# Node rows stored in the order of the edges, in a graph network of four layers

## The chip, the cores and the metric

The kernel runs on one core of a Trainium2 chip. The metric is the device time of one execution in microseconds (us). The engines are PE (matrix products), DVE (vector), ACT (activations), POOL (here above all the issuer of indirect DMAs) and SP, which issues plain DMAs. Data lies in HBM, and passes through SBUF (128 partitions) and PSUM.

## The reference

50,000 nodes with 256 numbers each, and 50,000 edges (src, dst), sorted by dst. Four layers follow each other, each with a residual and a layer norm.

```python
edge_index = jnp.stack([src, dst])
x = _layernorm(x + _L0(x, edge_index, edge_weight, W, b))        # 2 hops: msg = segment_sum(norm * h[src], dst); relu(h) @ W.T + b
x = _layernorm(x + _L1(x, ..., edge_attr_3, edge_index))         # attention over 8 heads, edge encoder dotted with h[dst]
x = _layernorm(x + _L2(x, edge_attr_64, src, dst, ...))          # attention, score = eh[src] + ee + et[dst]
x = _layernorm(x + _L3(x, edge_attr_20, ..., edge_index))        # filter, below
# L3: row, col = ei (so row = src and col = dst)
filt = silu(rbf @ Wf1 + bf1) @ Wf2 + bf2
agg = segment_sum(x[col] * filt, row)                            # x[dst], summed by src
h = silu(agg @ Wu1 + bu1) @ Wu2 + bu2
return x + (gamma * (h - mean) * rsqrt(var + 1e-5) + beta)       # mean and var over all nodes
```

## The kernel before

Nodes and edges are padded to NP = 128 x 392 and laid out as [P, C]: partition p holds C = 392 neighbouring rows. Every stage walks over the columns, G = 2 columns a slot (196 slots) or, in the attention, G = 4 columns a unit (98 units), through 4 or 7 buffers. Since edges are sorted by dst, the sum over the edges of one node is a running sum along a partition, and a small fix-up joins runs that cross partitions.

The stages are separate blocks with a barrier between them:

- `setup` (L153): loads, index vectors, degrees. Its last block (L360) works out `last_i`, the row of each node's last edge, and writes a small table beside x (`XT`, L436).
- `hop_edges(0)`, `hop_edges(1)` (L440): POOL gathers a row per edge (L480), DVE adds along the column (L541), SP stores the running sums.
- `layer_nodes(0..2)` (L622): for each node POOL gathers the finished sum by `last_i` (L673), SP loads x (L663), DVE adds bias, mixes and measures, ACT applies the norm (L616), PE turns and multiplies for the next table (L833). In layers 1 and 2 DVE first inverts the 16 denominators of a slot (L701, L705).
- `attention_edges(1)`, `(2)` (L844): for each of 4 columns POOL gathers the row of dst (L901) and that of src (L903). SP at step t issues the attributes of t (L877), the store of unit t-2 (L883), and a write of zeroes to one of the two tables that the filter adds into (L887); all are on one queue. DVE at step t scores t (L971 to L989; in layer 2 from L977) and sums t-1 (L1000 to L1007). PE encodes the attributes (L916), ACT rectifies and takes exponentials (L933).
- `filter_edges` (L1081): POOL gathers x[dst] (L1116) and, three slots later, adds messages into A[0] and A[1] by src (L1123); each pair of adds waits until that of the slot before has landed. Edges of one column with equal src are first joined by a product with an equality matrix (`eq`, L1195, and L1160 on PE); all but the first go to a trash row. PE computes the filter (L1137, L1151) and turns the src column (L1143), DVE compares and multiplies (L1195 to L1215).
- `update_nodes` (L1220): SP loads both tables, DVE adds them (L1300), PE turns and multiplies twice.
- `finish_nodes` (L1322): batch norm on ACT (L1368), x loaded by SP (L1343), sum, layer norm, store.

An engine executes its instructions in the order in which `unrolled` writes them: at step t each stage function in the list runs for slot t - lag. `hold(e, *done(stage, i, s, back))` waits until `stage` has finished the slot `back` before this one.

## Time and profile before

| what | value |
|---|---|
| median of 3 runs | 8170.37 us (8163.16 to 8176.74) |
| profiled execution | 8169.49 us |
| its span | 8167.8 us |
| busy share: PE, DVE, ACT, POOL | 52%, 65%, 40%, 58% |
| mean granted TensorE clock | 0.713 |
| HBM read, written | 968.89 MB, 840.95 MB |

The span runs from the first to the last instruction. A busy share is a mean over the stages, which have different limits, so a table by stage says more; its rows stand below. "DMA share" is the mean busy share of the 16 DMA engines, and PEld is PE's loading of weights. The first group shows eight stages, one a line: setup, attention 1, node stage 1, attention 2, node stage 2, filter, update, finish; in brackets stands how many instructions ran.

### The profile page before, as it was taken

To read this page: it belongs to the slowest core of one execution; us is meant where nothing else is said; L and a number is where in the kernel's file an instruction comes from. 1 tells how busy PE (TensorE), PEld (TensorE's weight loads), DVE (VectorE), ACT (ScalarE), POOL (GpSimd) and SP (SyncE) were. 2 spreads that over 40 slices of the span, in tenths; PEclk is the share of its full clock that TensorE was granted. 3 is DMA by queue.
4 is the path that set the end of the run, shared out by engine and by line. 5 is a ranking of instruction groups with operands and counts; after the bars stand their busy time and mean duration, and the time that the engine had idled before them with its cause. 6 is when DMAs were issued, how large, how long until landed. Compare 5 with 4: busy or idle time off the path is not lost. (4 is left out here: it accounts for less than half of the span.)

```text
span 8167.8 us, 82421 instructions
## 1 busy us (share of the span) xinstructions
PE 4280.0 (52%) x18128; PEld 3266.2 (40%) x18128; DVE 5331.3 (65%) x16616; ACT 3287.2 (40%) x8834; POOL 4767.5 (58%) x4730
## 2 busy tenths in 40 slices
PE   7800000799963333488511111003877877999854
PEld 4400000688852222366411111002555554888733
DVE  7856677677767777799744446997444444455577
ACT  4567300688851111388500001443222222444499
POOL 7777677544447777566577776666777777000000
PEclk9955555899975555699855555556888887999955
DMA  9299899777767677799755556886555554666699
GB/s 273 7 279 311 291 301 299 234 243 243 243 194 222 221 222 224 231 357 357 258 179 179 177 178 187 270 270 182 83 83 84 84 84 77 197 203 203 203 361 348
DMA packets 1128113, 1764.26 MB, mean 216 GB/s; under 512 B 247612, under 2 KB 606500, under 8 KB 1127626
## 3 DMA queue, kind: packets, MB, share of 16 engines
q1 hardware_dynamic: 641162, 903.37, 33.4%
q0 software_dynamic: 238720, 537.64, 26.8%
q10 hardware_dynamic: 247744, 318.00, 11.2%
q8 instruction: 154, 2.52, 0.1%
q14 instruction: 333, 2.73, 0.1%
HBM read 968.89 MB, written 840.95 MB: 222 GB/s over the span
## 5 line engine op out<-in xcount | busy, mean ns | idle before, releaser
L673 POOL DMA_INDIRECT st<-S,last_i x1176 | 1152.3, 980 | 872.8 <-DVE yt L714 364.7
L903 POOL DMA_INDIRECT rows<-T,src_i x784 | 749.4, 956 | 238.9 <-issue 238.9
L616 ACT ACTIVATE xo<-z,shift,rsd 128x256 f32<-128x256 f32 x1568 | 849.9, 593 | 0.5 <-issue 0.2
L1123 POOL DMA_INDIRECT A<-comb,ai x392 | 628.8, 1604 | 161.7 <-issue 135.7
L916 PE MATMUL psE<-encs,attr 4*128 4x256 f32 x784 | 369.7, 648 | 620.0 <-DMA attr<-in_attr3T 617.8
L933 ACT ACTIVATE psX<-diff 128x40 f32<-128x40 f32 x196 | 40.7, 208 | 1592.4 <-DVE diff L989 1592.4
L916 PE MATMUL psE<-fes,attr 64*128 64x8 f32 x784 | 183.3, 360 | 804.4 <-DMA attr<-in_attr64T 802.1
L1137 PE MATMUL psH<-rbf,wf1s 20*128 20x256 f32 x784 | 264.7, 464 | 603.3 <-DMA rbf<-in_rbfT 603.3
L1195 DVE TENSOR_SCALAR eq<-psI,src_f 128x128 f32<-128x128 f32 x392 | 136.8, 349 | 668.9 <-DMA A<-comb,ai 597.5
L565 PE MATMUL psC<-sums,chain 128*128 128x256 f32 x4 | 2.4, 700 | 1082.6 <-PEq L454 1082.6
L588 DVE BATCH_NORM_STATS2 row_stats<-z 128x6 f32<-128x256 f32 x1568 | 561.3, 400 | 0.1
L916 PEld LDWEIGHTS psE<-encs,attr 4*128 4x128 f32 x784 | 243.7, 325 | 745.7 <-DMA attr<-in_attr3T 686.7
L916 PEld LDWEIGHTS psE<-fes,attr 64*128 64x128 f32 x784 | 174.2, 325 | 813.8 <-DMA attr<-in_attr64T 811.5
L480 POOL DMA_INDIRECT rows<-XT,src_i x392 | 380.6, 971 | 171.1 <-issue 102.1
L1151 PE MATMUL psF<-wf2s,hid 128*128 128x256 f32 x1568 | 477.3, 460 | 0.0
L1116 POOL DMA_INDIRECT rows<-X,dst_i x392 | 391.0, 997 | 136.5 <-issue 118.8
L901 POOL DMA_INDIRECT rowsd<-T,dst_i x392 | 371.4, 947 | 168.2 <-issue 107.6
L480 POOL DMA_INDIRECT rows<-S,from_i x392 | 396.0, 1010 | 122.9 <-issue 100.3
L833 PE MATMUL psV<-w2s,xT 128*128 128x272 f32 x1568 | 407.7, 403 | 106.8 <-ACT tt L769 106.8
L1182 ACT COPY comb<-psM 128x512 f32<-128x512 f32 x196 | 114.9, 586 | 863.1 <-PE psM L1160 863.1
L901 POOL DMA_INDIRECT rowsd<-ET,dst_i x392 | 373.4, 952 | 149.4 <-issue 118.5
L565 PEld LDWEIGHTS psC<-sums,chain 128*128 128x128 f32 x4 | 1.0, 312 | 1083.3 <-issue 1083.3
(241 smaller groups left out, 14232.2 us busy)
## 6 DMA issues: line engine op xcount, KB each, us to landing
X<-xo ACTq DMA_DIRECT2D x588, 256.0 KB
xt<-X SPq DMA_DIRECT2D x588, 256.0 KB
S<-sums SPq DMA_DIRECT2D x196, 544.0 KB, 3.1
S<-sums SPq DMA_DIRECT2D x392, 256.0 KB, 3.9
A<-zero SPq DMA_DIRECT2D x196, 512.0 KB, 4.6
T<-tt ACTq DMA_DIRECT2D x196, 280.0 KB
T<-tt ACTq DMA_DIRECT2D x196, 272.0 KB
XT<-in_x SPq DMA_DIRECT2D x1, 50176.0 KB, 169.4
```

The costliest lines, as they stand in the source:

```text
L480: e.indirect_dma_start(rows[s][:, k, :], None, table, bass.IndirectOffsetOnAxis(ap=at_i[:, c:c + 1], axis=0))\
L588: ins = e.bn_stats(row_stats[s][:, k, :], z[s][:, k, :])
L616: ins = e.activation(y[s][:, k, :], z[s][:, k, :], ACT.Identity, bias=shift[s][:, k, :], scale=rsd[s][:, k, :])
L673: e.indirect_dma_start(st[s][:, k, :], None, sums_table, bass.IndirectOffsetOnAxis(ap=last_i[:, c:c + 1], axis=0))\
L833: mm = e.matmul(psV[k][:, 0:DW], xT[s][:, k, m * P:(m + 1) * P], weights[:, m, :], start=m == 0, stop=m == K - 1)
L901: e.indirect_dma_start(rowsd[s][:, k, :], None, dtable, bass.IndirectOffsetOnAxis(ap=dst_i[:, c:c + 1], axis=0))\
L903: e.indirect_dma_start(rows[s][:, k, :], None, table, bass.IndirectOffsetOnAxis(ap=src_i[:, c:c + 1], axis=0))\
L916: mm = e.matmul(psE[s % 2][:, k * EW:(k + 1) * EW], attr[s][:, k, :], weights[:], start=True, stop=True)
L1116: e.indirect_dma_start(rows[s][:, k, :], None, X3, bass.IndirectOffsetOnAxis(ap=dst_i[:, c:c + 1], axis=0))\
L1123: e.indirect_dma_start(A[k], bass.IndirectOffsetOnAxis(ap=ai[s][:, k, :], axis=0), comb[s][:, k, :], None, compute_op=ALU.add).then_inc(si ...
L1137: mm = e.matmul(psH[s % 2][:, m * G * P:(m + 1) * G * P], wf1s[:, m * P:(m + 1) * P], rbf[s][:].rearrange("p g q -> p (g q)"), start=True, ...
L1151: mm = e.matmul(psF[s % 2][:, k * D:(k + 1) * D], hid[s][:, m, k * P:(k + 1) * P], wf2s[:, m, :], start=m == 0, stop=m == K - 1)
```

## The change

Node rows are renumbered. Node v, where it has edges, is stored at the row of one of its own edges (the first in the tables between the hops and layer 1, the last from layer 1 on), and nodes without edges fill the rows that are left over. The sums of a node then already lie at the node's row: a stage over the nodes loads them plainly. In exchange x has to be brought into the order: it is gathered in node stage 0 (`input_i`), moved from first to last row in node stage 1 (`turn_i`), and taken back to the nodes' own order in `finish_nodes` (`node_i`). Which empty node takes which free row is worked out by a new block in `setup`, on DVE: for each of the two lists a `compress` (ten binary steps over 392 and ten over 784 numbers) and an `expand` (ten steps over 1568).

```diff
+                        def compress(j, flag, count):
...
+                            for b in reversed(range(BITS)):
+                                link(e.tensor_scalar(bit[:], rem[:], float(2 ** b), None, ALU.is_ge))
+                                e.scalar_tensor_tensor(rev[:], bit[:], float(2 ** (BITS - 1 - b)), rev[:], ALU.mult, ALU.add)
+                                link(e.scalar_tensor_tensor(rem[:], bit[:], -float(2 ** b), rem[:], ALU.mult, ALU.add))
...
+                            for b in range(BITS):
...
+                                e.tensor_scalar(moved[:, 0, :], a, top, 0.0, ALU.subtract, ALU.max)
+                                link(e.scalar_tensor_tensor(z, a, top, a, ALU.is_lt, ALU.mult))
+                                link(e.tensor_tensor(z[:, 0:W - d], z[:, 0:W - d], moved[:, 0, d:W], ALU.add))
+                        def expand(j, turn):
...
+                            for b in reversed(range(BITS)):
...
+                                e.tensor_scalar(moved[:], a[:], top, 0.0, ALU.subtract, ALU.max)
+                                link(e.scalar_tensor_tensor(z[:], a[:], top, a[:], ALU.is_lt, ALU.mult))
+                                if d < W:
+                                    link(e.tensor_tensor(z[:, :, d:W], z[:, :, d:W], moved[:, :, 0:W - d], ALU.add))
```

(W = 2 x 392. `link` makes DVE wait for the instruction before the next.) The table beside x gets two more columns, and the hops walk from the last column to the first.

The row of dst is no longer gathered per edge. In attention 1 the stored rows are loaded plainly, ACT sets those that are not at a first edge to zero, and DVE carries the row of the first edge along; the filter does the same from the last edge backwards. In attention 2 the 8 numbers are loaded once for all columns, multiplied, and spread by 8 scans at the start.

```diff
# attention_edges
+                        def take(i, s):
+                            hold(e, *done(spread_, i, s, NS - 1))
+                            e.dma_start(rowsd[s][:], nodes(T1)[:, bass.ds((i * NS + s) * G, G), :]).then_inc(signal(taken, s), 16)
+                        written(N, NS, ([(take, 0)] if layer == 1 else []) + [(stage, 0), (store, 2), (empty, 2)])
...
-                                e.indirect_dma_start(rowsd[s][:, k, :], None, dtable, bass.IndirectOffsetOnAxis(ap=dst_i[:, c:c + 1], axis=0))\
...
+                        def cut_rows(i, s):
+                            hold(e, *done(taken, i, s))
+                            for k in range(G):
+                                ins = e.activation(rowsd[s][:, k, :], rowsd[s][:, k, :], ACT.Copy, scale=isfirst[:, bass.ds((i * NS + s) * G + k, 1)])
...
+                        def spread_rows(i, s):
+                            hold(e, *done(cut, i, s))
+                            for k in range(G):
+                                c = (i * NS + s) * G + k
+                                last = rowsd[s][:, k - 1, :] if k else rowsd[(s - 1) % NS][:, G - 1, :] if i + s else head[:]
+                                ins = e.scalar_tensor_tensor(rowsd[s][:, k, :], last, notfirst[:, c:c + 1], rowsd[s][:, k, :], ALU.mult, ALU.add)
...
-                        written(N, NS, ([(rectify, 0)] if layer == 1 else []) + [(exponentials, 0), (keep_max, 0)])
+                        written(N, NS, ([(cut_rows, 0), (rectify, 0)] if layer == 1 else []) + [(exponentials, 1), (keep_max, 1)])
...
-                        written(N, NS, [(score, 0), (add, 1)])
+                        written(N, NS, ([(spread_rows, 0)] if layer == 1 else []) + [(score, 0), (add, 1)])
```

The filter adds into four tables instead of two: slot s uses A[0], A[1] when it is even and A[2], A[3] when it is odd, and each add waits for the same column two slots back. Each attention stage writes two tables of zeroes where it wrote one. The update loads four tables and adds them in pairs, in three sums a slot for one.

```diff
# filter_edges
-                            hold(e, *done(added, i, s, 1))
                             for k in range(G):
-                                e.indirect_dma_start(A[k], bass.IndirectOffsetOnAxis(ap=ai[s][:, k, :], axis=0), comb[s][:, k, :], None,
-                                                     compute_op=ALU.add).then_inc(signal(added, s), 16)
+                                hold(e, *done(added[k], i, s, 2))
+                                e.indirect_dma_start(A[s % 2 * 2 + k], bass.IndirectOffsetOnAxis(ap=ai[s][:, k, :], axis=0), comb[s][:, k, :], None,
+                                                     compute_op=ALU.add).then_inc(signal(added[k], s), 16)
-                        unrolled(R, NS, [(gather, 0), (add, LAG)])
+                        unrolled(R, NS, [(add, 0)])
...
-                        unrolled(R, NS, [(column, 0), (activate, 0), (copy, 2)])
+                        unrolled(R, NS, [(column, 0), (cut_rows, 0), (activate, 0), (copy, 2)])
-                        unrolled(R, NS, [(compare, 0), (multiply, 1)])
+                        unrolled(R, NS, [(spread_rows, 0), (compare, 0), (multiply, 1)])
# layer_nodes
-                            e.dma_start(xt[s][:], xin[:, c, :]).then_inc(signal(loaded, s), 16)
+                            e.dma_start(st[s][:], nodes(sums_table)[:, c, :]).then_inc(signal(loaded, s), 16)
...
+                        def cut(i, s):
+                            hold(e, *done(st_["weighed"], i, s))
+                            own = islast[:, bass.ds(i * (G * NS) + s * G, G)].rearrange("p (g h) -> p g h", h=1).to_broadcast([P, G, H])
+                            e.tensor_tensor(den[s], den[s], own, ALU.mult).then_inc(signal(st_["cut"], s), 1)
# update_nodes
+                            e.dma_start(third[s][:], nodes(A[2])[:, c, :]).then_inc(signal(loaded, s), 16)
+                            e.dma_start(fourth[s][:], nodes(A[3])[:, c, :]).then_inc(signal(loaded, s), 16)
...
-                        unrolled(R, NS, [(add, 0), (copy, 0), (measure, 3)])
+                        unrolled(R, NS, [(add, 0), (copy, 1), (pair, 0), (measure, 4)])
# finish_nodes
-                            e.dma_start(xt[s][:], nodes(X3)[:, bass.ds(i * (G * NS) + s * G, G), :]).then_inc(signal(loaded, s), 16)
+                                e.indirect_dma_start(xt[s][:, k, :], None, X3, bass.IndirectOffsetOnAxis(ap=node_i[:, c:c + 1], axis=0))\
```

## Rows read from the trace of the kernel before

**Rows 1.** Stages: length; busy PE, PEld, DVE, ACT, POOL; clock; DMA share; GB/s

```profile
0.00:421.00 421.00, 331.18 (x1204) 184.08 (x1204) 321.35 (x862) 206.01 (x395) 316.49 (x410) 0.94 0.59 137
...
2364.00:3394.00 1030.00, 377.19 (x816) 250.29 (x816) 737.29 (x1595) 143.66 (x395) 752.53 (x789) 0.50 0.68 214
3394.00:4015.00 621.00, 495.38 (x2352) 381.36 (x2352) 594.13 (x2156) 500.91 (x1569) 367.41 (x389) 0.98 1.01 344
4015.00:5041.00 1026.00, 190.85 (x816) 180.83 (x816) 494.16 (x1391) 40.18 (x200) 750.85 (x789) 0.50 0.56 172
5041.00:5633.00 592.00, 0.00 (x0) 0.00 (x0) 583.95 (x2156) 250.66 (x588) 368.02 (x390) 0.50 0.85 265
5633.00:6945.00 1312.00, 1025.27 (x3528) 704.89 (x3528) 589.10 (x2156) 298.76 (x785) 1019.80 (x784) 0.83 0.51 82
6945.00:7720.00 775.00, 765.80 (x3920) 673.90 (x3920) 383.82 (x784) 329.57 (x784) 0.00 (x0) 0.99 0.63 200
7720.00:8168.00 448.00, 218.22 (x784) 140.10 (x784) 339.77 (x1378) 426.87 (x982) 0.00 (x0) 0.50 0.98 345
```

**Rows 2.** Groups of instructions: busy, mean ns of one | idle before, releaser

```profile
L903 POOL DMA_INDIRECT rows<-T,src_i x784 | 749.4, 956 | 238.9 <-issue 238.9
L1123 POOL DMA_INDIRECT A<-comb,ai x392 | 628.8, 1604 | 161.7 <-issue 135.7 <-DMA A<-comb,ai 20.4 <-ACT comb L1182 5.7
...
L541 DVE SCALAR_TENSOR_TENSOR sums<-sums,same,rows 128x256 f32<-128x256 f32 x784 | 381.0, 486 | 21.6 <-issue 0.6
...
L496 ACT ACTIVATE xe<-rows,f 128x256 f32<-128x256 f32 x392 | 177.8, 500 | 91.3 <-DVE f L526 89.3
...
L701 DVE TENSOR_SCALAR psDen<-st 128x16 f32<-128x16 f32 x392 | 68.6, 175 | 12.7 <-DMA st<-S,last_i 12.7
```

**Rows 3.** Timeline (start us, length us) of the end of setup

```profile
387.88 0.57 DVE L408 TENSOR_TENSOR ahead<-ahead,w_sb 128x392 f32<-128x392 f32 x1
...
394.25 0.36 DVE L416 TENSOR_SCALAR g_dst<-ahead 128x392 f32<-128x392 f32 x1
...
421.74 1.20 POOL L480 DMA_INDIRECT rows<-XT,src_i  x1 [52.00 <-PEq L454]
```

**Rows 4.** Timeline of a unit of attention 1: score begins, last sums, next attributes usable

```profile
2801.56 1.23 DVE L971 TENSOR_TENSOR enc<-psE,rowsd 128x1024 f32<-128x1024 f32 x1 [3.61 <-DMA rows<-T,src_i]
...
2807.79 1.55 DVE L1007 SCALAR_TENSOR_TENSOR sums<-sums,same,rows 128x264 f32<-128x264 f32 x3
...
2814.49 2.07 PE L916 MATMUL psE<-encs,attr 4*128 4x256 f32 x4 [7.79 <-DMA attr<-in_attr3T]
```

**Rows 5.** DMA issues in attention 1: count, size, median us from issue to landing

```profile
S<-sums SPq DMA_DIRECT2D x74, 544.0 KB, 3.5
A<-zero SPq DMA_DIRECT2D x74, 512.0 KB, 4.7
```

**Rows 6.** Timeline of a unit of attention 2: the same three points

```profile
4501.98 0.19 DVE L977 TENSOR_TENSOR dot<-rows,rowsd 128x32 f32<-128x32 f32 x1 [5.66 <-DMA rows<-T,src_i]
...
4505.67 1.55 DVE L1007 SCALAR_TENSOR_TENSOR sums<-sums,same,rows 128x264 f32<-128x264 f32 x3
...
4513.17 1.02 PE L916 MATMUL psE<-fes,attr 64*128 64x8 f32 x4 [9.04 <-DMA attr<-in_attr64T]
```

**Rows 7.** Timeline of a slot of the filter, DVE and PE

```profile
6202.31 0.35 DVE L1195 TENSOR_SCALAR eq<-psI,src_f 128x128 f32<-128x128 f32 x1 [3.90 <-DMA A<-comb,ai]
...
6204.76 0.69 DVE L1215 TENSOR_TENSOR fl<-psF,rows 128x512 f32<-128x512 f32 x1
...
6205.50 1.13 PE L1160 MATMUL psM<-fl,eq 128*128 128x256 f32 x4 [2.76 <-DVE fl L1215]
...
6206.56 1.13 PE L1137 MATMUL psH<-rbf,wf1s 20*128 20x256 f32 x4
...
6207.62 0.43 PE L1143 MATMUL psI<-ident,sc 128*128 128x128 f32 x2
...
6207.89 1.89 PE L1151 MATMUL psF<-wf2s,hid 128*128 128x256 f32 x8
```

More of the change, by code:

```diff
@@ new lines, in setup @@
+                assert W <= 1024 and C < 512
+                rowid, free, empty, frees, empties = [tmp(n, [P, C]) for n in ("rowid", "free", "empty", "frees", "empties")]
+                firsts, lasts = tmp("firsts", [P, C]), tmp("lasts", [P, C])
+                below = tmp("below", [P, 2])
+                deg, ok, dinv, sq = tmp("deg", [P, C]), tmp("ok", [P, C]), tmp("dinv", [P, C]), tmp("sq", [P, C])
+                degr, okr, root = tmp("degr", [P, C]), tmp("okr", [P, C]), tmp("root", [P, C])
@@ L381, in _ @@
                         link(e.tensor_tensor_scan(number[:], unit[:], psNum[:, 0:C], 0.0, ALU.mult, ALU.add))
+                        link(e.tensor_tensor(firsts[:], number[:], psNum[:, 0:C], ALU.subtract))
+                        link(e.tensor_scalar(empty[:], has[:], -1.0, 1.0, ALU.mult, ALU.add))
+                        link(e.tensor_tensor_scan(empties[:], unit[:], empty[:], 0.0, ALU.mult, ALU.add))
+                        link(e.tensor_tensor_scan(frees[:], unit[:], notfirst[:], 0.0, ALU.mult, ALU.add))
                         assert n[0] == NUMBER
@@ L564, in _ @@
                     def _(e):
-                        e.matmul(ps[:], chain[:], sums[NS - 1][:, G - 1, :], start=True, stop=True).then_inc(carried, 1)
+                        e.matmul(ps[:], chainT[:], sums[NS - 1][:, 0, :], start=True, stop=True).then_inc(carried, 1)
                     @block.gpsimd
                     def _(e):
-                        at = bass.IndirectOffsetOnAxis(ap=first_e[:], axis=0)
+                        at = bass.IndirectOffsetOnAxis(ap=start_e[:], axis=0)
                         e.wait_ge(cleared, 1)
@@ L1093, in filter_edges @@
                 psH, psI, psF, psM = [[bank(f"{n}{j}") for j in range(2)] for n in ("psH", "psI", "psF", "psM")]
-                gathered, added, attred = stage_of("gathered", NS, G), stage_of("added", NS, G), stage_of("attred", NS, 1)
+                tail = ctx.enter_context(sbuf("tail", [P, D], F32))
+                taken, attred = stage_of("taken", NS, 1), stage_of("attred", NS, 1)
+                added = [stage_of(f"added{k}", NS, 1) for k in range(G)]
+                cut, spread_ = stage_of("cut", NS), stage_of("spread", NS)
+                csteps, ends = semaphore("csteps"), semaphore("ends")
                 stages = [stage_of(n, NS) for n in (
@@ L1110, in _ @@
+                        unrolled(R, NS, [(take, 0), (stage, 0)])
                     @block.gpsimd
                     def _(e):
-                        def gather(i, s):
-                            hold(e, *done(message, i, s, NS))
-                            for k in range(G):
-                                c = i * (G * NS) + s * G + k
-                                e.indirect_dma_start(rows[s][:, k, :], None, X3, bass.IndirectOffsetOnAxis(ap=dst_i[:, c:c + 1], axis=0))\
-                                    .then_inc(signal(gathered, s), 16)
@@ L1128, in _ @@
+                        unrolled(R, NS, [(add, 0)])
+                        for sem, value in total(added[0], R) + total(added[1], R):
                             e.wait_ge(sem, value)
@@ L1180, in copy, with cut_rows @@
                             hold(e, *done(joined, i, s))
-                            hold(e, *done(added, i, s, NS))
+                            hold(e, *done(added[0], i, s, NS))
+                            hold(e, *done(added[1], i, s, NS))
                             e.copy(comb[s][:].rearrange("p g d -> p (g d)"), psM[s % 2][:]).then_inc(signal(copied, s), 1)
-                        unrolled(R, NS, [(column, 0), (activate, 0), (copy, 2)])
+                        def cut_rows(i, s):
+                            hold(e, *done(taken, i, s))
+                            for k in range(G):
+                                ins = e.activation(rows[s][:, k, :], rows[s][:, k, :], ACT.Copy, scale=islast[:, bass.ds(C - (i * NS + s + 1) * G + k, 1)])
+                            ins.then_inc(signal(cut, s), 1)
+                        unrolled(R, NS, [(column, 0), (cut_rows, 0), (activate, 0), (copy, 2)])
                     @block.vector
@@ L1206, in compare, with spread_rows @@
                             e.tensor_scalar(ai[s][:], cnt[s][:], trash[:], None, ALU.add).then_inc(signal(compared, s), 1)
+                        def spread_rows(i, s):
+                            hold(e, *done(cut, i, s))
+                            for k in reversed(range(G)):
+                                c = C - (i * NS + s + 1) * G + k
+                                last = rows[s][:, k + 1, :] if k < G - 1 else rows[(s - 1) % NS][:, 0, :] if i + s else tail[:]
+                                ins = e.scalar_tensor_tensor(rows[s][:, k, :], last, notlast[:, c:c + 1], rows[s][:, k, :], ALU.mult, ALU.add)
+                                if k:
+                                    ins.then_inc(csteps, 1)
+                                    e.wait_ge(csteps, (i * NS + s) * (G - 1) + G - k)
+                            ins.then_inc(signal(spread_, s), 1)
                         def multiply(i, s):
```

426 lines of the change are left out of this document (322 added, 104 removed).

## The prediction, made before the changed kernel ran

> **What bounds the kernel now.** I read first the table of stages [rows 1], because the stages are separate blocks and each has its own limit. Setup (421 us) is vector work and PE counting. The hops and the first node stage (421 to 2364 us, left out of the rows) are paced by row gathers and by PE; nothing in them is removed. The two attention stages take 1030 and 1026 us, and POOL is busy for 750 us in each although DVE differs by 240 us: POOL sets both. The two later node stages (621 and 592 us) have DVE busy for 594 and 584 us: DVE sets them. The filter stage (1312 us) has POOL busy for 1020 us. The update has PE busy for 766 of 775 us. In finish ACT is busy for 427 of 448 us and the DMA engines move 345 GB/s.
>
> Then I read what one POOL operation costs with its issue gap [rows 2]: a gather is 0.96 us plus 0.30 us of issue, so 1.26 us each; an accumulating scatter is 1.60 plus 0.3 us. An attention unit has 8 gathers: 8 x 1.26 = 10.05 us, and 98 units are 985 us of the 1030. A filter slot has 2 gathers and 2 scatters: 2.5 + 3.9 = 6.4 us, against 1312/196 = 6.7. So the change attacks what really binds there. By the code POOL's indirect DMAs fall from 11 x 392 to 8 x 392, but 392 of those left are new in a stage that had none.
>
> The sum is made against the profiled execution (8169.5 us, 1.7 us of it outside the span); the median shown is 8170.4 us, so no correction is needed. This kernel's timing tells a change from none at about 0.2%, 16 us.
>
> **Setup, +207 us.** A new block works out the free rows, on DVE alone, one instruction waiting for the last. [rows 3] gives the prices: 0.57 us for a two-operand instruction over 392 elements (spaced 0.60), 0.36 us for a one-operand one (0.40). The larger part is loops that compress or spread a list in ten binary steps. I scale with length at about 1.04 ns an element for two operands and half that for one: an estimate from those rows. One compress: 30 instructions over 392 (15 us), 30 over 784 or less (24 us), 8 more (4 us) = 43 us, twice: 86. One expand: 10 steps over 1568 elements (0.9 + 1.8 + 1.6 us) = 43 us and 12 shorter ones (9 us) = 52, twice: 105. The rest, some 45 instructions and the PE round trips, 29 us. That is 220. Added in the older blocks: 20 more instructions, 13 us. Against that, the hop started 27 us after DVE's last instruction, because the small table was still being written [rows 3]; now it is written during the second expand, and those 26 us go. 220 + 13 - 26 = 207. Bounds 185 and 235.
>
> **Hops and node stage 0, 0.** The order of columns is turned round and index copies are three columns wide, with the same gathers of the same bytes. In node stage 0 the gather moves from the sums to x; PE stays full. Bounds -5 and +10.
>
> **Attention 1, +14 us.** Half of the gathers go: POOL needs 5.0 us per unit. What is late next? DVE: from enc to the last sum it takes 2809.34 - 2801.56 = 7.78 us [rows 4], and it gets four carried multiply-adds over 280 elements; three over 264 take 1.55 us, so four take 2.1: 9.95 us per unit. So the relief is nearly nothing here. Beside it, there is a loop through SP's queue. At the end of unit t-2's sum, SP issues the store, then two zero writes (one before), then the load of the rows for t+1. A tiny load behind one store and one zero write was usable at 2814.49, 5.15 us after DVE's end [rows 4]; a store lands 3.5 us after its issue and a zero write, issued some 0.4 us behind it, 4.7 us [rows 5], so each further half megabyte costs 1.6 us. The new load is usable at 5.15 + 1.6 + 1.6 = 8.4 us; ACT then scales four rows, 0.50 us each with some overlap [rows 2]: 10.3 us. DVE's step is 9.95, and the loop spans two steps: (9.95 + 10.3)/2 = 10.1, I take 10.2. 97 x 10.2 + 55 (what the stage has outside its units now) = 1044. Bounds -10 (9.95) and +125.
>
> The Trainium skill (DMA: Bandwidth & Descriptors, Queues, rings and completion order) says that descriptors of one queue are consumed in ring order on each engine; the late tiny load agrees. Were the load free to pass the writes, the unit would be DVE's 9.95 us and the stage 1020.
>
> **Attention 2, -249 us.** No carried rows here: the destination's 8 numbers are spread once for all. DVE's chain is 4501.98 to 4507.22, 5.24 us [rows 6]; POOL 5.0. But bytes per unit are 0.56 MB gathered, 0.56 stored, 1.05 zeroes, 0.13 attributes, 2.29 MB. Now the stage moves 172 GB/s at a DMA share of 0.56 [rows 1], 307 GB/s at a full share; node stage 1 shows 344 at 1.01. So 2.29 MB take 6.7 to 7.5 us: the engines bind before DVE. The loop: attributes were usable 5.95 us after DVE's end (4513.17) [rows 6], plus 1.75 for the second zero write, plus 1.9 us of PE = 9.6; (5.24 + 9.6)/2 = 7.4 us. 97 x 7.4 + 51 + 8 (the spreading at the start: a multiply and eight scans, partly behind the first gathers) = 777. Bounds 738 (7.0 us) and 870.
>
> **Node stages 1 and 2, +43 us each.** The gathers that go were not binding. DVE gets one small multiply on 16 numbers in PSUM with a wait behind it: the neighbouring 16-number operation takes 0.175 us [rows 2], and wait and drain add 0.04: 0.22 x 196 = 43. Nothing hides it, since DVE is busy for 96 to 99% of both. Bounds 25 and 60 each.
>
> **Filter, -404 us.** POOL keeps two scatters, 3.9 us a slot, and with four tables a scatter waits for the same column two slots back rather than one. Next are PE and DVE. PE's starts in a slot [rows 7]: from join to hide 1.06, hide to transpose 1.06, transpose to filter 0.27, the filter 1.89: 4.28 us. DVE: 6202.31 to 6205.45 = 3.14 us [rows 7], plus two carried adds of 0.485 each [rows 2] = 4.15. The ring of four buffers (compare, the next step's multiply, join, copy, two scatters and a landing) I estimate at 15 us over 4 slots, 3.75 a slot. With three engines within 0.4 us of each other I take 4.5, not 4.3. 196 x 4.5 + 26 = 908. Bounds: 869 (4.3) and 1053 (5.24).
>
> The carried adds have two SBUF inputs, and POOL reads indices from SBUF. The Trainium skill (SBUF — State Buffer, on the port pair shared by DVE and GpSimd) says that such a DVE operation and a GpSimd operation that reads SBUF exclude each other for a whole instruction. In attention 1 now, with such sums on DVE, gathers keep to a mean of 0.96 us [rows 2]. By the rule each scatter could wait 0.5 us, 4.9 us a slot and 986 for the stage; I go by the row.
>
> **Update, +36 us.** Loads double: 1.31 MB per slot with the store, and PE's slot is 3.9 us. By the stage's own rate (200 GB/s at 0.63, 317 at a full share [rows 1]) they take 4.1 us; by node stage 1's 344 GB/s they take 3.8. I take 4.08: 800 + 11 = 811. DVE gets two more sums of 0.68 us (scaled as in setup), 384/196 + 1.4 = 3.4 of 3.9 us in all, and stays below. Bounds 0 and +95.
>
> **Finish, +61 us.** x now comes by 392 gathers at 1.26 us = 494 us; they start with the block, and from the last to the stored row I estimate 14 us: 509 instead of 448. POOL takes ACT's place as the bound. Bounds 50 and 85.
>
> **Sum.** 207 + 14 - 249 + 43 + 43 - 404 + 36 + 61 = -249: 8169.5 - 249 = 7920 us.
>
> **Rivals.** A: the filter doesn't get to 4.5. PE's granted clock is 0.83 there [rows 1], below full speed; if it stays so, 4.28/0.83 = 5.16 us a slot, 1037 for the stage, 8050 in all. For: 0.83 with PE busy 78%. Against: node stage 1 has 0.98 at 80%, and PE would be nearly full.
>
> B, slower than before: the added bytes cost more than the gathers saved. The attention stages get 103 MB more of zeroes, the update 103 MB more of loads. If mixed reading and writing stays at 270 GB/s, attention 1 takes 11.3 us a unit (+107 on my sum), attention 2 8.5 (+107), the update 4.85 (+151), finish 2.9 (+77): 8362. It decides below about 288 GB/s. For: attention 2 manages 307 per full share. Against: node stage 1 and finish show 344 and 345 GB/s in fact.
>
> C: everything sits on its engine's floor, 4.3, 7.0, 9.95 and 3.9 us: 138 us less, 7782.
>
> D: the gathers that go weren't what bound attention 2 and the filter, and the stages keep their length: 8169.5 + 404 = 8573. The 0.30 us gaps between POOL's operations speak against it; I give it 0.02.
>
> **How the numbers follow.** Forecast 0.57, A 0.19, C 0.12, B 0.10, D 0.02. The forecast's own range is 7850 to 8000. The range reaches to C and past A, and into the way to B: 7790 to 8130. Slower: B and D, 0.12. Same: 0.03, the point where B just eats the gain. Faster: 0.85.
>
> **What would show it.** Setup ends near 628 us; enc starts follow each other by 10.2 us in attention 1 and the first dot by 7.4 in attention 2, with DVE waiting for attributes; mix starts 3.25 us apart in node stages 1 and 2; filter slots are 4.5 us with a granted clock near 1 and POOL waiting for comb; POOL is the engine without idle time in finish. I am wrong if setup's chain is spaced otherwise, if the filter waits for its scatters' landing, or if attention 2 stays above 8 us a unit.

## The result, and the profile after

The changed kernel takes 8085.51 us (median of 4 runs, 8070.34 to 8096.18) against 8166.76 us for the kernel before, run beside it (4 runs, 8162.18 to 8176.74): ratio 0.9897, 95% interval 0.9878 to 0.9917. It is faster by 81 us or 1.0%, a third of the 249 us that were forecast, and inside the range. The profiled execution took 8096.18 us, its span 8094.3 us, so its stages add up to 73 us less than before.

The first view is the table of stages of the changed kernel, with the columns of [rows 1] and its order of stages: setup, attention 1, node stage 1, attention 2, node stage 2, filter, update, finish.

```profile
0.00:629.00 629.00, 351.17 (x1244) 194.63 (x1244) 536.97 (x1154) 206.56 (x396) 321.53 (x412) 0.82 0.40 93
...
2579.00:3729.00 1150.00, 377.20 (x816) 250.22 (x816) 934.00 (x1982) 309.13 (x787) 387.70 (x395) 0.50 0.69 236
3729.00:4377.00 648.00, 512.42 (x2352) 367.44 (x2352) 621.64 (x2357) 481.34 (x1569) 370.80 (x392) 0.98 1.00 330
4377.00:5178.00 801.00, 190.80 (x816) 180.78 (x816) 503.74 (x1400) 39.10 (x199) 377.60 (x395) 0.50 0.87 284
5178.00:5817.00 639.00, 0.00 (x0) 0.00 (x0) 621.31 (x2353) 252.22 (x590) 0.97 (x1) 0.50 0.77 247
5817.00:6625.00 808.00, 792.03 (x3528) 592.44 (x3528) 752.76 (x2548) 434.80 (x1176) 613.30 (x392) 0.99 0.80 133
6625.00:7589.00 964.00, 815.04 (x3920) 672.33 (x3920) 619.11 (x1177) 329.41 (x785) 0.00 (x0) 0.97 0.82 267
7589.00:8094.00 505.00, 218.35 (x784) 140.25 (x784) 354.52 (x1378) 437.82 (x982) 371.11 (x392) 0.50 0.94 306
```

Length against [rows 1], in us:

| stage | before | forecast | after | moved by |
|---|---|---|---|---|
| setup | 421 | +207 | 629 | +208 |
| hops and node stage 0 | 1943 | 0 | 1950 | +7 |
| attention 1 | 1030 | +14 | 1150 | +120 |
| node stages 1, 2 | 621, 592 | +43, +43 | 648, 639 | +27, +47 |
| attention 2 | 1026 | -249 | 801 | -225 |
| filter | 1312 | -404 | 808 | -504 |
| update | 775 | +36 | 964 | +189 |
| finish | 448 | +61 | 505 | +57 |

Two stages miss badly, attention 1 by 106 us and the update by 153. The filter gives 100 us of it back: without that luck the kernel would take some 8185 us, outside the range and slower than before. In the two stages that miss no engine is full: DVE is busy for 934 of 1150 us, PE for 815 of 964, and the DMA engines for 0.69 and 0.82. So a wait sets them. The timelines show which. First a unit of attention 1 after (start, length, idle before it and its releaser):

```profile
3002.82 1.55 DVE L1268 SCALAR_TENSOR_TENSOR sums<-sums,same,rows 128x264 f32<-128x264 f32 x3
3003.54 1.78 ACT L1160 ACTIVATE rowsd<-rowsd,isfirst 128x280 f32<-128x280 f32 x4 [6.76 <-DMA rowsd<-T]
...
3003.79 3.78 PE L1143 MATMUL psE<-encs,attr 4*128 4x256 f32 x8 [8.39 <-DMA attr<-in_attr3T]
3004.40 0.33 SPq L1101 DMA_DIRECT2D S<-sums  x1
3004.64 0.94 POOL L1126 DMA_INDIRECT rows<-T,index_i  x1 [5.43 <-DVE sums L1268]
3004.77 1.46 SPq L1106 DMA_DIRECT2D A<-zero  x2
...
3006.27 1.41 SPq L1111 DMA_DIRECT2D rowsd<-T  x1
...
3007.60 1.07 ACT L1154 ACTIVATE psE<-psE 128x512 f32<-128x512 f32 x2 [2.28 <-PE psE L1143]
...
3008.80 1.22 DVE L1232 TENSOR_TENSOR enc<-psE,rowsd 128x1024 f32<-128x1024 f32 x1 [1.18 <-ACT psX L1166]
...
3014.14 1.78 ACT L1160 ACTIVATE rowsd<-rowsd,isfirst 128x280 f32<-128x280 f32 x4 [5.20 <-DMA rowsd<-T]
...
3014.60 3.77 PE L1143 MATMUL psE<-encs,attr 4*128 4x256 f32 x8 [7.04 <-DMA attr<-in_attr3T]
```

POOL idles for 5.43 us, as it should with half of the gathers gone. ACT idles for 6.76 us until the rows of dst have landed. Their load waits on SP's queue for DVE's end (3004.37), then follows the store and both zero writes. It has landed at 3014.14, 9.8 us after DVE's end; over 75 units the median is 9.5 us (8.9 to 10.7). The forecast had 8.4. The attributes of the same unit stand behind the rows on the queue: they reach PE a little later (3014.60 here, 9.9 us after DVE's end in the median). PE and ACT then need 4.9 us to encode and rectify them (3003.79 to 3008.67 for the unit shown), and DVE's score (`enc`, L1232) waits for that: it starts 0.13 us after L1154 has ended, and by the code it is `rectified` that it waits for, though the view names the exponentials.

The update, in the same view:

```profile
7003.65 0.84 ACT L1579 ACTIVATE ht<-psO,bu2s 128x256 f32<-128x256 f32 x2 [0.89 <-PE psO L1550]
...
7004.52 0.52 SPq L1531 DMA_DIRECT2D HT<-ht  x1
7005.08 0.61 SPq L1524 DMA_DIRECT2D agg<-A  x1
...
7005.73 0.45 SPq L1525 DMA_DIRECT2D more<-A  x1
...
7005.92 0.69 DVE L1588 TENSOR_TENSOR agg<-agg,more 128x512 f32<-128x512 f32 x1 [1.70 <-DMA fourth<-A]
...
7006.70 0.43 SPq L1527 DMA_DIRECT2D fourth<-A  x1
```

SP issues the store of slot t-4 the moment ACT has written it (7003.65 + 0.84 = 7004.49), and only then the four loads of a later slot. DVE then waits for the last of them. The view of waits sums this over the 800 us from 6700 to 7500 (us in total, times, longest):

```profile
DVE agg L1588 <- DMA fourth<-A: 277.7, 161, 5.6
```

### The profile page after: what moved, and what is told of

Same layout as the page of the kernel before. It is cut to its first block and busy times, and to the rows that moved or that the text cites. A ratio compares the mean times of both kernels' runs of the same rounds, so it can differ in the third digit from the quotient of the medians.

```text
span 8094.3 us, 85002 instructions
## 1 busy us (share of the span) xinstructions
PE 4133.3 (51%) x18168; PEld 3149.1 (39%) x18168; DVE 6231.1 (77%) x18486; ACT 3581.9 (44%) x9619; POOL 3605.0 (45%) x3559
## 3 DMA queue, kind: packets, MB, share of 16 engines
q10 hardware_dynamic: 247744, 318.00, 11.3%
## 5 line engine op out<-in xcount | busy, mean ns | idle before, releaser
L1126 POOL DMA_INDIRECT rows<-T,index_i x784 | 759.3, 969 | 1080.8 <-DVE sums L1268 895.1
L1644 POOL DMA_INDIRECT xt<-X,node_i x392 | 371.1, 947 | 1095.1 <-POOLq L1711 971.5
L879 POOL DMA_INDIRECT xt<-in_x,input_i x392 | 376.6, 961 | 469.5 <-DVE xb L894 393.4
L801 ACT ACTIVATE sd<-mean_var,epsc 128x2 f32<-128x2 f32 x784 | 238.0, 304 | 582.3 <-DVE mean_var L796 578.6
L879 POOL DMA_INDIRECT xt<-X,turn_i x392 | 370.8, 946 | 251.1 <-DVE xb L894 184.1
L681 POOL DMA_INDIRECT rows<-S,index_i x392 | 401.6, 1025 | 122.8 <-issue 101.1
L959 ACT ACTIVATE yt<-yt,m_half 128x256 f32<-128x256 f32 x392 | 183.2, 532 | 565.2 <-DVE yt L925 565.2
L1160 ACT ACTIVATE rowsd<-rowsd,isfirst 128x280 f32<-128x280 f32 x392 | 174.9, 516 | 582.0 <-DMA rowsd<-T 582.0
L1402 PEld LDWEIGHTS psH<-rbf,wf1s 20*128 20x128 f32 x784 | 130.8, 185 | 722.0 <-DMA rbf<-in_rbfT 644.7
L1588 DVE TENSOR_TENSOR agg<-agg,more 128x512 f32<-128x512 f32 x196 | 135.6, 692 | 346.7 <-DMA fourth<-A 346.0
```

Source lines behind the costliest of these rows:

```text
L681: e.indirect_dma_start(rows[s][:, k, :], None, table, bass.IndirectOffsetOnAxis(ap=at_i[:, c:c + 1], axis=0))\
L801: e.activation(sd[s][:, :, 0], mean_var[s][:, :, 1], ACT.Sqrt, bias=epsc[:]).then_inc(signal(rooted, s), 1)
L879: e.indirect_dma_start(xt[s][:, k, :], None, xin, bass.IndirectOffsetOnAxis(ap=at_i[:, c:c + 1], axis=0))\
L959: ins = e.activation(yt[s][:, k, :], yt[s][:, k, :], ACT.Relu, scale=m_half[:, bass.ds(i * (G * NS) + (s * G + k), 1)])
L1126: e.indirect_dma_start(rows[s][:, k, :], None, table, bass.IndirectOffsetOnAxis(ap=at_i[:, c:c + 1], axis=0))\
L1402: mm = e.matmul(psH[s % 2][:, m * G * P:(m + 1) * G * P], wf1s[:, m * P:(m + 1) * P], rbf[s][:].rearrange("p g q -> p (g q)"), start=True, ...
```

## The experiments

All are edits of the changed kernel except the one that edits the kernel before. They fall into two settings, by what the kernel before took beside them: 8165 to 8167 us (the first setting) or 8587 to 8589 us (the second). Whether the chip makes the setting is taken up at the end. A time without a number of runs is that of a single run. I read the length of a unit or slot from first and last start of one DVE instruction (98 units: divided by 97; 196 slots: by 195). For the changed kernel itself that view says, for attention 1, attention 2, filter and update:

```profile
L1232 DVE TENSOR_TENSOR enc<-psE,rowsd x98: 1223/1224/1226, 2595.1 to 3691.7; 128x1024 f32<-128x1024 f32 x98
L1239 DVE TENSOR_TENSOR dot<-dot,psE x98: 186/186/189, 4404.4 to 5143.3; 128x32 f32<-128x32 f32 x98
L1499 DVE TENSOR_TENSOR fl<-psF,rows x196: 690/692/692, 5827.4 to 6609.6; 128x512 f32<-128x512 f32 x196
L1588 DVE TENSOR_TENSOR agg<-agg,more x196: 682/692/694, 6631.5 to 7572.8; 128x512 f32<-128x512 f32 x196
```

That is 11.31, 7.62, 4.01 and 4.83 us.

**The update's store two slots later.**

```diff
-                        unrolled(R, NS, [(load, 0), (store, 4)])
+                        unrolled(R, NS, [(load, 0), (store, 6)])
```

> Update only: the store of slot t-6 instead of t-4 stands behind the load of t in SP's order, so that a load no longer waits until the result of a slot two steps further on is ready. Theory 'order': the update is 4.85 us a slot because SP is held at the store; it falls to 4.1 or less, the stage from 964 to about 810 us and the run by some 150 us. Rival 'rate': five transfers of 256 KB a slot move at 272 GB/s at most in this mix, whoever issues them; the stage stays at 964 within 10 us.

Measured: 7914.57 us (one run, the kernel before 8166.79 beside it). The same starts in the update:

```profile
L1588 DVE TENSOR_TENSOR agg<-agg,more x196: 671/675/693, 6633.4 to 7388.9; 128x512 f32<-128x512 f32 x196
```

3.87 us a slot instead of 4.83, with every byte as before. From 6640 to 7380 us PE has no idle time and the DMA engines move 338 GB/s:

```profile
6640.00:7380.00 740.00, 740.00 (x3797) 653.05 (x3796) 597.67 (x1140) 318.04 (x758) 0.00 (x0) 1.00 0.98 338
```

So the order on the queue cost 0.96 us a slot, 187 us by the slots (171 by the whole time), and the rate nothing.

**The third and fourth table loaded by ACT's queue**, store as in the changed kernel:

```diff
-                            e.dma_start(third[s][:], nodes(A[2])[:, c, :]).then_inc(signal(loaded, s), 16)
-                            e.dma_start(fourth[s][:], nodes(A[3])[:, c, :]).then_inc(signal(loaded, s), 16)
...
-                        unrolled(R, NS, [(activate, 1), (bias, 2)])
+                        unrolled(R, NS, [(load_more, 0), (activate, 5), (bias, 6)])
```

(`load_more` issues the two loads from ACT.)

> Update only: the third and fourth tables are loaded by ACT, through a second queue, with activate and bias at lags 5 and 6 so that the loads are as early as SP's; the store stays at lag 4 on SP. Theory 'order': ACT's two loads come early but SP's two are still held, 4.5 to 4.85 us a slot, 890 to 960 us. Rival 'one queue': a single queue cannot fill the 16 DMA engines (its share is 0.83), two can; 4.1 us, about 810 us. Rival 'rate': 964 us as after the change.

Measured: 8036.39 us, the update 4.53 us a slot. It gains 0.30 us of 0.96: two loads are free of the store, the other two still stand behind it. The store's place counts, more than the number of queues. (ACT's own work had to move to lags 5 and 6 for this, so the queue is not all that differs.)

**Attention's store and zero writes one unit later.**

```diff
-                        written(N, NS, ([(take, 0)] if layer == 1 else []) + [(stage, 0), (store, 2), (empty, 2)])
+                        written(N, NS, ([(take, 0)] if layer == 1 else []) + [(stage, 0), (store, 3), (empty, 3)])
```

> Attention stages only: store and zero writes of unit t-3 instead of t-2 follow the loads of t in SP's order, so that the load of the next unit's rows is issued one step of DVE earlier. Theory 'loop': the stages are set by the loop store, two zero writes, load, and then ACT or PE; with a step more of distance attention 1 falls to DVE's 10.0 us a unit (1150 to about 1030 us) and attention 2 from 7.7 to the DMA engines' 7.0 (801 to about 735). Rival 'rate': the DMA engines cannot move the bytes faster in this mix; both stages stay within 15 us of 1150 and 801.

Measured: 7769.75 us. Starts in attention 1 and 2:

```profile
L1232 DVE TENSOR_TENSOR enc<-psE,rowsd x98: 1223/1224/1225, 2590.7 to 3553.6; 128x1024 f32<-128x1024 f32 x98
L1239 DVE TENSOR_TENSOR dot<-dot,psE x98: 186/186/189, 4266.5 to 4831.4; 128x32 f32<-128x32 f32 x98
```

Attention 1 is 9.93 us a unit, which is DVE's chain of 9.95 in the forecast; the rows still land 9.6 us after the store is issued, but now a unit earlier than they are needed. Attention 2 is 5.82 us, below the 6.7 to 7.5 that the forecast held for the DMA engines' floor. From 4270 to 4830 us they moved

```profile
4270.00:4830.00 560.00, 176.60 (x756) 167.80 (x757) 470.36 (x1334) 35.60 (x190) 356.49 (x376) 0.50 1.05 387
```

387 GB/s. The stage had never been short of rate.

**Zero writes from ACT's queue**, with the old lag of two:

```diff
-                        written(N, NS, ([(take, 0)] if layer == 1 else []) + [(stage, 0), (store, 2), (empty, 2)])
+                        written(N, NS, ([(take, 0)] if layer == 1 else []) + [(stage, 0), (store, 2)])
...
-                        written(N, NS, ([(cut_rows, 0), (rectify, 0)] if layer == 1 else []) + [(exponentials, 1), (keep_max, 1)])
+                        written(N, NS, ([(cut_rows, 0), (rectify, 0)] if layer == 1 else []) + [(exponentials, 1), (keep_max, 1), (empty, 2)])
```

> The changed kernel with attention's zero writes issued from ACT's queue instead of SP's, same lag of two units, same bytes. Theory (the carried-row load waits behind the zero writes because they are on one queue): attention 1 falls from 11.3 to 10.0 to 10.4 us a unit, attention 2 from 7.6 to 6.9 or less, about 8085 - 110 - 70 = 7905. Rival (the DMA engines are short of rate for those bytes wherever they are issued): 11.3 and 7.6 stay, 8085. Should ACT's own work be held up by its issuing, attention 1 would rise above 11.3.

Measured: 8069.28 us, in the second setting, where the kernel before takes 8587. The starts there:

```profile
L1232 DVE TENSOR_TENSOR enc<-psE,rowsd x98: 1223/1224/1225, 2699.0 to 3689.4; 128x1024 f32<-128x1024 f32 x98
L1239 DVE TENSOR_TENSOR dot<-dot,psE x98: 186/186/189, 4401.9 to 5014.6; 128x32 f32<-128x32 f32 x98
```

10.21 and 6.32 us a unit: with the same bytes and the same lag, taking two writes from the queue ahead of the load gives 1.10 us back in attention 1 and 1.30 in attention 2. Rate can't do that. The changed kernel's 11.31 and 7.62 are from the first setting; that can't make the gain, since the one version measured in both (both stores late, below) takes 9.94 and 5.93 us in the second and 9.93 and 5.83 in the first. The expected 7905 was for the first setting.

**Two tables instead of four**: the filter adds as before (each add waits for the same column one slot back), attention writes one table of zeroes per unit, the update loads two.

```diff
-                                hold(e, *done(added[k], i, s, 2))
-                                e.indirect_dma_start(A[s % 2 * 2 + k], bass.IndirectOffsetOnAxis(ap=ai[s][:, k, :], axis=0), comb[s][:, k, :], None,
+                                hold(e, *done(added[k], i, s, 1))
+                                e.indirect_dma_start(A[k], bass.IndirectOffsetOnAxis(ap=ai[s][:, k, :], axis=0), comb[s][:, k, :], None,
```

> Two tables instead of four, the rest of the change kept: each add waits for the same column's add one slot back, the attention stages write one table of zeroes each, the update loads two tables and adds them once. Theory: the four tables were not what freed the filter (the gathers' going was): a landing of 4.0 us and 0.2 of issue allow 4.2 to 4.5 us a slot, the filter takes 840 to 900 us (808 with four), while the update returns to 775 (from 964), attention 1 to 1030 to 1060 and attention 2 to 700 to 740; the run is about 7800 us. Rival: with one pair in flight the adds wait for each other's landing, 5.9 us a slot or more, the filter is back above 1150 us and the run is no faster than 8050.

Measured: 7851.87 us, faster than the change as it was made. Attention 1 is 10.18 us a unit, attention 2 6.66, the filter 4.76 a slot, the update 3.88. In the filter the wait for the landing of the add before comes back; first the waits from 5630 to 6530 us here, then those of the changed kernel from 5830 to 6600:

```profile
POOL A L1387 <- DMA A<-comb,ai: 230.0, 184, 2.1
PEld psM L1425 <- DVE fl L1499: 145.6, 164, 3.6
```

```profile
POOL A L1387 <- DMA A<-comb,ai: 68.3, 118, 0.7
...
PEld psM L1425 <- DVE fl L1499: 3.1, 12, 0.6
```

The filter missed its expected 840 to 900 us: 929 pass between its first and last start alone. Before, a slot was 6.52 us (6915.6 - 5644.8, by 195), so the rest of the change, the gathers' going above all, is worth 1.76 us a slot and the two extra tables 0.75, 147 us. At their first price (110 us in attention 1, 93 in attention 2, 185 in the update) they lost 241 net; the attention part is queueing only.

**Both cures together**, and with two tables:

> The changed kernel with both cures: attention's store and zero writes three units behind instead of two, the update's store six slots behind instead of four. Theory (both stages were held by what stands ahead of the next load on SP's queue, and the two are separate): the gains add up, attention 1 at 9.9 us a unit, attention 2 at 5.8, filter 4.0, update 3.87, so 8085 - 316 - 171 = 7600 us, 7570 to 7630. Rival (the shortened stages take something from each other, or the single looks were lucky): above 7700. Rival from the forecast (the DMA engines' rate sets attention 2 at 6.7 to 7.5 and the update at 4.1 or more): at least 7790.

> As the run before with both stores late, but with the filter adding into two tables as the kernel before does (each add waits for the same column one slot back, one zero write per attention unit, two loads in the update). It prices the four tables once their queueing is cured. Theory: filter 4.76 instead of 4.0 us a slot (+147 us), attention 2 a little below 5.8 (at most 50 us less), attention 1 at DVE's 9.9, update 3.87: 7600 + 147 - 50 = 7700, 7680 to 7760. Rival (the two extra tables cost as much traffic as they save, as without the cure): within 40 us of the run before.

These ran in the second setting: 7820.94 us (5 runs, 7805.67 to 7822.34), ratio 0.9108 (0.9095 to 0.9120), and 7951.76 us (5 runs), ratio 0.9266 (0.9253 to 0.9278); the kernel before 8586.7 (12 runs). The stages named were as expected (9.94, 5.93, 4.02 and 3.87 us; filter 4.75 with two tables). So, once nothing queues, four tables are worth 131 us, and the filter alone differs. The absolute times missed because of the setting. The first again, beside the changed kernel:

> The changed kernel with both stores late, once more, since the last comparison ran where the kernel before took 8587 us instead of 8167 (its row gathers stalled). Theory: where the kernel before takes about 8167 us, this takes 7600 us (7570 to 7630), ratio 0.931; where it takes about 8587, 7820 again, ratio 0.911.

> The changed kernel itself, beside the run before it on one chip, to compare the two directly. Theory: where the kernel before takes 8167 us, 8085, ratio 0.990; where it takes about 8587, about 8300 (7820 plus 316 and 171), ratio 0.967: the gathers that the change removes are those that stall there.

Measured in the first setting, where the kernel before takes 8164.81 us (9 runs): both stores late 7600.91 (5 runs, 7598.3 to 7612.0), ratio 0.9311 (0.9299 to 0.9324); the changed kernel 8081.98 (4 runs), ratio 0.9897 (0.9882 to 0.9912). The cures add up: 481 us.

**The kernel before with the same lags.**

> The kernel before with the same two lags (attention store and zero write 3 units behind, update store 6 slots behind). Theory: nothing, 8167 within 0.3%, since POOL's eight gathers set both attention stages and PE's 3.9 us the update, and the loads were early enough there. Rival (the lags are a gain of their own, and the cured kernel's win is not that of the change): attention or update shorter by over 30 us.

Measured: 8562.57 us (median of 7 runs) against 8586.7, ratio 0.9973 (0.9960 to 0.9986): 24 us, small but clear, against 481 in the changed kernel. So nearly all of the gain needs the shortened stages. The update is 3.88 us a slot, as in the kernel before. For attention it is less certain: this ran in the second setting alone, where the kernel before left no trace, so which stage gave the 24 us isn't shown.

That run also tells what is different in the second setting. POOL's gathers of dst in attention 1, in the view of [rows 2] (mean 955 ns, 947 in the same group of the kernel before in the first setting):

```profile
L901 POOL DMA_INDIRECT rowsd<-T,dst_i x392 | 374.4, 955 | 306.7 <-DVE sums L1007 146.1 <-issue 111.5 <-POOLq L1408 49.0
```

The issue costs the same, but POOL waits 146.1 us for buffers that DVE hasn't freed (11.6 in the first setting). DVE in turn waits for DMAs before its sums (L1003: 145.8 us in 36 gaps), which it hardly does in the first setting: rows land late. In the finish stage of the run with both stores late it is seen singly:

```profile
7496.09 0.69 DVE L1703 SCALAR_TENSOR_TENSOR z<-xt,psN 128x512 f32<-128x512 f32 x1 [1.58 <-issue]
7503.27 0.69 DVE L1703 SCALAR_TENSOR_TENSOR z<-xt,psN 128x512 f32<-128x512 f32 x1 [3.27 <-DMA A<-comb,ai]
7504.94 0.66 DVE L1703 SCALAR_TENSOR_TENSOR z<-xt,psN 128x512 f32<-128x512 f32 x1
```

Between two sums 7.2 us pass instead of 1.6 to 2.5; a gap of over one and a half medians comes 38 times in 195 steps there, 27 of them over 5 us, and 3 times (none over 5 us) in the same kernel's run in the first setting. Hops, attention before and finish after lose by it (attention 1 before: 11.63 us a unit instead of 10.05; finish after: 577 us between first and last sum instead of 483). The filter and the update don't, and the cured attention hardly does (5.93 for 5.83 us in attention 2).

**The cut of the denominators left out** (so nodes without edges get wrong rows), on top of both late stores:

```diff
-                                  + ([(cut, 0), (mix, 0)] if layer else []))
+                                  + ([(mix, 0)] if layer else []))
```

> As the first of these three, but the small multiplication of the 16 inverted denominators by the has-edges flag (node stages 1 and 2) is left out, so nodes without edges get wrong rows. Theory (the forecast's step: one DVE operation of 0.175 us and its wait, on an engine without idle time): node stages 1 and 2 shorter by 43 us each. Rival (the stages' 27 and 47 us more came from something else, the plain loads or x's gathers): shorter by less than 20 us each.

Measured: 7528.05 us. One DVE instruction of attention 2 and one of the filter, with both stores late and then without the cut:

```profile
L1239 DVE TENSOR_TENSOR dot<-dot,psE x98: 186/186/190, 4268.0 to 4833.2; 128x32 f32<-128x32 f32 x98
L1499 DVE TENSOR_TENSOR fl<-psF,rows x196: 690/691/693, 5517.9 to 6298.5; 128x512 f32<-128x512 f32 x196
```

```profile
L1239 DVE TENSOR_TENSOR dot<-dot,psE x98: 186/186/190, 4239.8 to 4802.6; 128x32 f32<-128x32 f32 x98
L1499 DVE TENSOR_TENSOR fl<-psF,rows x196: 690/691/692, 5444.0 to 6224.8; 128x512 f32<-128x512 f32 x196
```

The first start in attention 2 comes 28 us earlier, which is node stage 1. Node stage 2 lies between the last start in attention 2 and the first in the filter: 684.7 us (5517.9 - 4833.2) and 641.4 us (5444.0 - 4802.6), 43 less.

**The cut folded into the bound**, a version that computes everything:

```diff
+                            e.tensor_scalar(least[:], notlast[:], 1e30, 1e-10, ALU.mult, ALU.add)
...
-                            e.tensor_scalar(den[s], v[:, :, :, HD], 1e-10, None, ALU.max).then_inc(signal(st_["combined"], s), 1)
+                            low = least[:, bass.ds(i * (G * NS) + s * G, G)].rearrange("p (g h) -> p g h", h=1).to_broadcast([P, G, H])
+                            e.tensor_tensor(den[s], v[:, :, :, HD], low, ALU.max).then_inc(signal(st_["combined"], s), 1)
```

> The changed kernel with both stores late, and the cut of the denominators folded into the operation before it: the lower bound 1e-10 becomes a column of numbers that is 1e-10 where a node has edges and 1e30 elsewhere, so the inverse is practically zero there and the multiplication goes. Theory (what a look without that multiplication gave, 28 and 45 us, is all regained, the other operation costs the same 0.175 us): where the kernel before takes 8165 us, 7601 - 73 = 7528, 7510 to 7550. Rival (a second operand from SBUF makes the first operation dearer, by up to what the multiplication cost): 7600.

Measured: 7753.11 us (4 runs, 7745.62 to 7756.72) in the second setting, where the kernel before takes 8588.65, ratio 0.9025 (0.9008 to 0.9043). Against both stores late in that setting (7820.94 us, measured another time) that is 68 us less where 73 were expected. It is the fastest version that computes everything; in the first setting it wasn't run. The operation with a second operand costs what the one-operand one did, 0.174 us:

```profile
L910 DVE TENSOR_TENSOR psDen<-st,least 128x16 f32<-128x16 f32 x392 | 68.4, 174 | 4.0 <-DMA st<-S 4.0
```

## Where the forecast was right, and where it failed

The forecast as a whole failed: 81 us came where it had 249. It failed in attention 1 and in the update, and the cause is the same in both: what stands ahead of a load on SP's queue. That the time lies in the range is luck, since the filter's error of 100 us has the other sign.

**Setup, hops, node stage 0, finish: right.** Counting the dependent DVE instructions and scaling [rows 3] with length gave 207 us for setup; it is 208. Finish is POOL's 392 gathers at 1.26 us, +57 for +61.

**Attention 1: two failed steps, and each is about half of the miss.** The loop through SP's queue over two units is right, but a term is too small and the path is not the longest one.

- *"so each further half megabyte costs 1.6 us. The new load is usable at ... 8.4 us".* It is usable 9.5 us after DVE's end. The price was a difference of two landings [rows 5]. With one zero write less (two tables) the rows are usable after 7.5 us, so a half megabyte costs 2.1 us (0.52 MB at 250 GB/s), and two such on 5.15 make 9.3. Why 2.1 and not 1.6 stays open. With 9.5 in place of 8.4 the forecast's equation gives 10.7 us a unit.
- *"ACT then scales four rows ... 10.3 us"*, after which only DVE's 9.95 follow. The loop doesn't close there but through the attributes, which now stand behind the new load: 9.9 us until PE can start, 4.9 for PE and ACT's rectifying, 0.1, and 7.8 from the score to the last sum, 22.7 us for two units, 11.35 a unit; 11.31 is measured. The sum left this path out. With one zero write the same sum is 7.6 + 4.9 + 0.1 + 7.8 = 20.4, 10.2 a unit, for the measured 10.18; by the path through ACT's scaling it would be the 9.95 of DVE.

The fall-back in that paragraph, DVE's 9.95, was right (9.93 with the late store). Its upper bound, +125, held 120. The Trainium skill's rule named there, that descriptors of one queue are taken in ring order (DMA: Bandwidth & Descriptors, Queues, rings and completion order), agrees with the run that issued the zero writes from another queue: 10.21.

**Update: the failed step is "by the stage's own rate they take 4.1 us ... I take 4.08".** I priced only bytes over rate. The rate was even better than I took (338 GB/s, all loads inside PE's 3.87 us). What I left out was the order on SP's queue, for which I had the code: a store that waits for its result stands ahead of the next loads. Before, two loads had time enough behind it, and with two tables and the same lag the slot is 3.88 us again; with four, issued one after another (the fourth starts 1.6 us after the first) and landing behind 0.26 MB of store, they come late. The stage got 189 us longer, twice my upper bound.

**Attention 2: right in its loop, wrong in its floor.** -225 for -249, and 7.62 for 7.4 us a unit. The loop through SP's queue was the right limit and nearly the right size: attributes at PE 8.0 us after the store's issue (7.7 forecast), 2.0 for PE, 5.25 for DVE, half of which is 7.6. The floor beside it, 6.7 to 7.5 us by rate, does not exist: the late store ran at 5.82, close to DVE's 5.24.

**Filter: mechanism right, size off by 100 us.** PE became the bound, at a granted clock of 0.99, so rival A is refuted. The term "PE: 4.28 us" was too large, mostly because its last part took the filter's modelled length (1.89) for the distance to the next start. In the changed kernel:

```profile
6202.63 1.03 PE L1425 MATMUL psM<-fl,eq 128*128 128x256 f32 x4
...
6203.59 1.13 PE L1402 MATMUL psH<-rbf,wf1s 20*128 20x256 f32 x4
...
6204.64 0.43 PE L1408 MATMUL psI<-ident,sc 128*128 128x128 f32 x2
...
6204.91 1.89 PE L1416 MATMUL psF<-wf2s,hid 128*128 128x256 f32 x8
...
6206.64 1.10 PE L1425 MATMUL psM<-fl,eq 128*128 128x256 f32 x4
```

From 6204.91 to 6206.64 are 1.73 us, 0.16 less, and from join to hide (6202.63 to 6203.59) 0.96 instead of 1.06; the whole slot is 4.01. The 0.2 us that I added because three engines were close to each other never came: DVE has 0.49 us of carried adds twice and still keeps up. Its 4.15 us a slot were too many as well; it is busy for 753 us of the stage, 3.8 a slot. The exclusion that the Trainium skill describes (SBUF — State Buffer, SBUF: two separate sides) isn't seen here. 392 scatters took 1.565 us on average beside the carried adds, 1.604 before [rows 2], and single ones overlap them without either getting longer:

```profile
6206.41 1.55 POOL L1387 DMA_INDIRECT A<-comb,ai  x1 [0.30 <-issue]
6206.47 0.47 DVE L1486 SCALAR_TENSOR_TENSOR rows<-rows,notlast,rows 128x256 f32<-128x256 f32 x1
```

```profile
L1387 POOL DMA_INDIRECT A<-comb,ai x392 | 613.3, 1565 | 188.2 <-DMA A<-comb,ai 69.2 <-issue 61.0 <-ACT comb L1448 58.1
```

**Node stages: right, from the price of one operation.** 27 and 47 us for twice 43; leaving it out gave back 28 and 43, so the cut is all of it in stage 1 and nearly all in stage 2. Stage 1 was forecast 16 us too long. That node stage 1 pays less fits its start, where something else than DVE was the last (594 of 621 us busy in [rows 1], 584 of 592 in stage 2); this is argued, not shown.

**Rival B** (270 GB/s of mixed traffic) had attention 1 at 11.3 and the update at 4.85, which is just what came, 11.31 and 4.83. It is still refuted: both fall to 9.93 and 3.87 with every byte in place, and the update then moves 338 GB/s and attention 2 387, where it wanted 270. Its 11.3 doesn't even follow from its rate: with the late store attention 1 moves 273 GB/s over 963 us, about 2.7 MB a unit, which at 270 GB/s is 10 us. A rival's number that fits does not show its mechanism. C came nearest to what is possible: its 9.95 and 3.9 are reached with two lags changed. D is refuted by the filter and attention 2.

## What to carry to other kernels

When loads or writes are added to a queue, write down what stands ahead of the next load, and what that one waits for. A store that waits for its result, issued ahead of a prefetch, ties the prefetch to the end of the pipeline, and it shows only once the stage has become short enough. A shorter step makes the same lag in slots a shorter lag in time, so the lags are to be set anew after each gain; here two lags were worth 481 us, six times the change itself. When a large load is put ahead of a small one on a queue, add up the path of the small one too, to the instruction of the full engine that needs it. The distance between starts of a busy engine is its price, not the modelled length of the last instruction.

## What the runs showed of the hardware that was not expected

- Rows gathered by index can come late through a whole comparison. In the second setting the kernel before takes 8587 us instead of 8165, at nearly the same mean granted clock (0.721 and 0.727 in the kernel with both stores late); some rows land several us late, and the ratio of one and the same kernel is 0.9108 there and 0.9311 in the first. That it is the chip isn't shown: the runs that name a chip name 0 and 9 in the first setting, 13 and again 0 in the second (8166.79 us, and later 8588.65, both under number 0).
- Attention 2 with the late store moves 387 GB/s, with gathers, stores and zero writes mixed; the best row before was 345 [rows 1]. Extrapolating a rate by the DMA share (307 GB/s at a full share) gave a fifth too little.
- A load of 0.57 MB behind a store and two half-megabyte writes on one queue is usable 9.5 us after the first was issued (median of 75), 7.5 us with one such write; the same bytes of zeroes on another queue took 1.1 us off each unit.
